# DMA transposes in place of TensorE transposes for most quantized rows of a feed-forward part, and the down product half a step later

## The reference, cut to what matters

```python
def _act_quant(x):
    scale = 127.0 / jnp.clip(jnp.max(jnp.abs(x), axis=-1, keepdims=True), 0.0001, None)
    y = jnp.clip(jnp.round(x * scale), -128, 127) / scale
    return x + jax.lax.stop_gradient(y - x)

def _linear_bit(x, w, g):
    xq = _act_quant(_rmsnorm(x, g))          # g * x * rsqrt(mean(x*x) + 1e-8)
    wq = _ternary_quant(w)
    return jnp.einsum('bsd,od->bso', xq, wq)

swish = jax.nn.silu(_linear_bit(x, w1, g1))   # w1, w2: 2048 x 512
h = swish * _linear_bit(x, w2, g2)
return _linear_bit(h, w3, g3)                 # w3: 512 x 2048
# around it: x = x + tanh(g_ffn[0]) * ffn(layernorm(x))
```

## Time and profile before

| | us |
|---|---|
| median of 3 runs (lowest to highest) | 655.0 (654.78 to 655.46) |
| the profiled execution | 656.19 |
| its span, first to last instruction | 654.4 |
| busy: TensorE / VectorE / ScalarE / GpSimd | 635.1 / 536.5 / 422.2 / 360.2 |
| HBM read / written | 45.16 MB / 2.10 MB |

### The profile page before, as it was taken

One profiled execution on the slowest core, in us unless ns is written; L12 is line 12 of the kernel. 1 busy time (PEld: TensorE's weight loads), 2 busy tenths in 40 slices (PEclk: granted clock), 3 DMA queues, 4 the chain that ended last, 5 costly groups with the idle time before them and its releaser, 6 DMA issues.

```text
span 654.4 us, 9986 instructions
## 1 busy us (share of the span) xinstructions
PE 635.1 (97%) x2968; PEld 394.0 (60%) x2968; DVE 536.5 (82%) x870; ACT 422.2 (65%) x693; POOL 360.2 (55%) x304
## 2 busy tenths in 40 slices
PE   8789999999999999999999999999999998999997
PEld 7555466766766676666666666566656554545553
DVE  4778787788878877887789978997899987998863
ACT  2564686477737764776567766776666633598875
POOL 4722376655545554565367854664457144686651
PEclk9999999999999999999999999999999999999999
DMA  8207976788589858984988798878689872000001
GB/s 283 87 6 188 274 196 164 206 223 240 151 227 241 219 131 239 251 224 106 251 222 221 201 242 224 222 195 231 169 221 251 198 177 81 1 1 33 17 35 48
DMA packets 45208, 112.79 MB, mean 172 GB/s; under 512 B 11888, under 2 KB 15088, under 8 KB 45040
## 3 DMA queue, kind: packets, MB, share of 16 engines
q1 hardware_dynamic: 42128, 104.24, 60.1%
q10 hardware_dynamic: 2976, 8.06, 4.0%
q0 software_dynamic: 64, 0.00, 0.0%
HBM read 45.16 MB, written 2.10 MB: 72 GB/s over the span
## 4 chain that ended last, share of the span: by engine, by line
PE 68%; DVE 10%; SPq 8%; ACT 4%; issue 4%; DMA 3%; POOL 1%; PEld 1%; POOLq 0%; ACTq 0%; DVEq 0%; PEldq 0%
PE ps_s L1443 11%; SPq L1132 8%; PE ps_b L1476 6%; PE ps_s L623 5%; PE ps_ctx L1476 5%; PE ps_b L1339 4%; PE ps_b L1394 4%; DMA G<-E 3%; PE ps_b L1341 3%; PE ps_b L1413 3%; PE ps_b L1340 3%; ACT E L1675 2%; PE ps_b L674 2%; DVE small L1858 2%; PE ps_ctx L1472 2%
## 5 line engine op out<-in xcount | busy, mean ns | idle before, releaser
L1675 ACT ACTIVATE E<-ps_s,small 128x1024 f32<-128x1024 f32 x128 | 142.5, 1116 | 143.4 <-DVE small L1858 110.5
L1241 POOL TENSOR_TENSOR G_lo<-G,g_hi 128x512 fp32r<-128x512 f32 x130 | 168.0, 1306 | 117.7 <-ACT g_hi L1619 117.7
L1858 DVE TENSOR_REDUCE small<-ps_s 128x1 f32<-128x1024 f32 x128 | 149.8, 1211 | 34.5 <-PE ps_s L1443 34.3
L1872 DVE STREAM_TRANSPOSE E<-E 128x1024 f32<-128x1024 f32 x124 | 152.0, 1230 | 0.1
L1199 POOL TENSOR_SCALAR E<-E,small 128x1024 f32<-128x1024 f32 x64 | 78.9, 1233 | 109.6 <-DVE small L1864 98.0
L1619 ACT ACTIVATE g_hi<-G 128x512 fp32r<-128x512 f32 x130 | 76.9, 631 | 3.5 <-DVE wq L1888 3.5
L1339 PE MATMUL ps_b<-b_hi,ctx_hi 128*128 128x512 f32 x128 | 66.8, 522 | 0.3 <-DVE ctx_lo L1818 0.3
L1476 PE MATMUL ps_b<-G,kv 128*128 128x512 f32 x126 | 63.7, 600 | 1.7 <-DMA G<-E 1.7
L1476 PE MATMUL ps_ctx<-G,kv 128*128 128x512 f32 x126 | 64.6, 607 | 0.1
L1443 PE MATMUL ps_s<-k_hi,q_hi 64*128 64x512 f32 x256 | 57.3, 444 | 3.8 <-ACT E L1675 2.6
L623 PE MATMUL ps_s<-wq,q12T 128*128 128x512 fp8e4 x256 | 59.8, 379 | 0.1
(11 more groups left out here) (203 smaller groups left out, 1211.7 us busy)
## 6 DMA issues: line engine op xcount, KB each, us to landing
G<-E SPq DMA_DIRECT2D x496, 128.0 KB, 2.6
w_stage<-in_wffn SPq DMA_DIRECT2D x37, 512.0 KB, 4.8
w_stage<-in_wffn ACTq DMA_DIRECT2D x11, 512.0 KB, 4.4
wo_s<-in_woT SPq DMA_DIRECT2D x8, 512.0 KB, 5.4
wq_s<-in_wq SPq DMA_DIRECT2D x7, 512.0 KB, 5.5
wkcq_s<-in_wkcqT SPq DMA_DIRECT2D x7, 384.0 KB, 3.4
out<-x_sb SPq DMA_DIRECT2D x8, 256.0 KB, 2.0
x_sb<-in_x SPq DMA_DIRECT2D x3, 512.0 KB, 6.3
```

Of the source, the lines that this page charges most:

```text
L1241: nc.gpsimd.tensor_tensor(g_tile(w % 2, i, G_lo), tile, high_part(i).bitcast(F32).rearrange("p (t i q) -> p t i q", t=ST, i=4), ALU.subtra ...
L1675: nc.scalar.activation(out, scores, ACT.Exp, bias=negmax[:, k:k + 1], accum_out=rowsum[:, k:k + 1]).then_inc(exp_done, 1)
L1858: nc.vector.tensor_reduce(negmax[:, k:k + 1], ps_s[:, t % 2, :], AX_X, ALU.max, negate=True).then_inc(max_done, 1)
L1872: nc.vector.transpose(e_tile(w % 2, t), e_tile(w % 2, t)).then_inc(blocks_turned, 1)
```

## The change

Rows of tiles 2 to 7 and hidden rows of tiles 0 to 5 are no longer turned by TensorE. ScalarE widens the integers to bfloat16 in place (`widen_rows`, 1024 columns, where the copy of turned rows stood; `widen_hidden`, 2048 columns, right behind the rounding and ahead of the square), and SyncE issues one transposing transfer within SBUF for each (`turn_rows`, `turn_hidden`), in the order rows 2, rows 3, hidden 0, rows 4, hidden 1, and so on, with the stores between them. The down product of tile `t - 3` stands after chunk 1 of step `t`; before, that of tile `t - 2` stood at the end of step `t`. VectorE's read of it moves from the end of its step to the place ahead of product 3. The tail is turned on TensorE as before. The scales `h_deq` get a column for each tile.

```diff
+            def turn_rows(t):
+                sp.wait_ge(q12_wide, t - FIRST_MOVED + 1)
+                sp.wait_ge(up_done, HC * (t - 1))
+                sp.dma_start_transpose(q12T[:, t % 2, :, :, :].rearrange("p i c s -> p (i c) s"),
+                                       qn12[:, t % 2, :, :].rearrange("p i d -> p (i d)").bitcast(BF16)).then_inc(q12_moved[t % 2], 16)
+            def turn_hidden(t):
+                sp.wait_ge(q3_wide, t + 1)
+                if t >= 2:
+                    sp.wait_ge(mm3_done, t - 1)
+                sp.dma_start_transpose(q3T[:, t % 2, :, :], qn3[:, t % 2, :].bitcast(BF16)).then_inc(q3_moved[t % 2], 16)
+            for t in range(1, TT):
+                if t + 1 < TT:
+                    turn_rows(t + 1)
+                if t >= 2:
+                    turn_hidden(t - 2)
+                if t >= 4:
+                    store(t - 4)
...
         def gate_up(pe, t, k, c):
-            pe.wait_ge(q12T_ready, 2 if early and c == 1 else t + 1)
+            if t < FIRST_MOVED:
+                pe.wait_ge(q12T_ready, 2 if early and c == 1 else t + 1)
+            else:
+                pe.wait_ge(q12_moved[t % 2], 16 * (t // 2))
...
-                    if turn and c == 0:
-                        turn_rows(pe, t, k)
-                    if out and c in T3_AT:
...
-                            last = nc.tensor.transpose(t3[:, a, b, :], qn3[:, k, (8 * a + b) * P:(8 * a + b + 1) * P].bitcast(BF16), identb[:, :])
-                if out and not (isinstance(t, int) and t == LAST):
...
+                    if t >= 3 and c == DOWN_AT:
+                        down(t - 3)
+            def down(t):
+                pe.wait_ge(q3_moved[t % 2], 16 * (t // 2 + 1))
+                pe.wait_ge(side_read, t + SIDE_READ0)
+                for f in range(FF // P):
...
+        def widen_rows(act, t):
+            act.wait_ge(q12_ready, t + 1)
+            rows = qn12[:, t % 2, :, :].rearrange("p i d -> p (i d)")
+            copy_act(rows.bitcast(BF16), rows).then_inc(q12_wide, 1)
+        def widen_hidden(act, t):
+            act.wait_ge(q3_ready, t + 1)
+            rows = qn3[:, t % 2, :]
+            copy_act(rows.bitcast(BF16), rows).then_inc(q3_wide, 1)
...
                     if turn and c == 0:
-                        turned_rows(act, t, k)
-                    if out and c in T3_AT:
...
+                        widen_rows(act, t + 1)
...
                 if t == 1:
                     silu(act, 2, 0, 0)
+                    widen_hidden(act, 0)
                     norm_act(act, 2, 0)
-                elif mm:
+                else:
+                    widen_hidden(act, t - 1)
                     hidden_square(act, t, k)
...
                     chunk_max(dve, t, k, 1)
+                    down_read(t - 3)
                     product(dve, t, k, 3)
```

More of the change, by code:

```diff
@@ L528, in ffn_sp, with store @@
             sp.dma_start(g3, A["g3"].partition_broadcast(P)).then_inc(ld_g3, 16)
-            with sp.Fori(0, TT) as t:
+            def store(t):
                 sp.wait_ge(side_read, t + (SIDE_READ0 + 1))
-                sp.dma_start(out_dram[:, bass.ds(t, 1), :], x_sb[:, bass.ds(t, 1), :]).then_inc(stored, 16)
+                sp.dma_start(out_dram[:, t:t + 1, :], x_sb[:, t:t + 1, :]).then_inc(stored, 16)
+            def turn_rows(t):
[15 more added lines that the diff above has]
+                    store(t - 4)
+            for t in range(LAST_MOVED - 1, TT):
+                store(t)
             sp.wait_ge(stored, 16 * TT)
@@ L658, in step @@
                             pe_last_out(pe, s)
-                    if turn and c == 0:
-                        turn_rows(pe, t, k)
-                    if out and c in T3_AT:
[L662 to L666, removed]
-                            last = nc.tensor.transpose(t3[:, a, b, :], qn3[:, k, (8 * a + b) * P:(8 * a + b + 1) * P].bitcast(BF16), identb[:, :])
-                        last.then_inc(t3_done, 1)
-                if out and not (isinstance(t, int) and t == LAST):
[L670 to L676, removed]
+                    if t >= 3 and c == DOWN_AT:
[4 more added lines that the diff above has]
+                for f in range(FF // P):
+                    last = nc.tensor.matmul(ps_side, q3T[:, t % 2, f, :], wq8[:, 2 * DT + f // 4, (f % 4) * NF:(f % 4 + 1) * NF],
+                                            start=(f == 0), stop=(f == FF // P - 1))
+                last.then_inc(mm3_done, 1)
             def turn_half(t, a):
                 pe.wait_ge(q3_half, 2 * (t - (LAST - 1)) + a + 1)
-                pe.wait_ge(et_free, 2 * t + (a - 1 + ET_FREE0))
+                pe.wait_ge(et_free, ET_FREE0 + (a + 1 if t == LAST else 0))
                 for b in range(8):
@@ L790, in step @@
                 if quant:
-                    if not (isinstance(t, int) and t < 3):
-                        act.wait_ge(t3_done, 2 * t - 4)
+                    if t >= 3:
+                        act.wait_ge(q3_moved[(t - 3) % 2], 16 * ((t - 3) // 2 + 1))
                     act.wait_ge(hfac_chain, HCH * t)
@@ L932, in norm_quant @@
             scales(dve, y_am[:, 2 * k:2 * k + 2], fs[:, bass.ds(t + 10, 1)], y_fac[:, 2 * k:2 * k + 2], yfac_chain, 3 * t + 6)
-            if not (isinstance(t, int) and t < 0):
+            if 0 <= t < FIRST_MOVED:
                 dve.wait_ge(t12_done, t + 1)
+            elif t >= FIRST_MOVED:
+                dve.wait_ge(q12_moved[t % 2], 16 * (t // 2))
             for i in range(2):
@@ L1079, in step @@
                     chunk_max(dve, t, k, 3)
-                if out and not (isinstance(t, int) and t == LAST):
-                    dve.wait_ge(mm3_done, t - 1)
-                    dve.wait_ge(hdeq_ready, t - 1)
-                    x = x_tile(t - 2)
-                    nc.vector.scalar_tensor_tensor(x, ps_side, h_deq[:, k:k + 1], x, ALU.mult, ALU.add).then_inc(side_read, 1)
             product(dve, 0, 0, 3)
```

31 lines of the change are left out of this document (14 added, 17 removed).

## The result

| | before | after |
|---|---|---|
| median of the runs, us | 654.89 (653.38 to 655.46, 6 runs) | 659.46 (657.49 to 659.85, 6 runs) |
| ratio, 95% interval | | 1.0066 (1.0051 to 1.0081) |
| profiled execution: time, span, us | 656.19, 654.4 | 659.71, 657.9 |
| TensorE busy, us | 635.1 | 628.1 |

The account below looks back on a forecast made before the run. TensorE's 11.70 us step was taken as the bound, with a ring of 11.58 through GpSimd, VectorE and ScalarE just under it. Terms +2.6, +1.2 and +1.3 sum to +5.1, taken as +5.0 on 655.0: 660.0 us, range 656.5 to 668.

Parts of the forecast that it names:

- The bound: Feed-forward steps: TensorE, busy in all 11.70 us, drops to 10.37 a step and disappears under the ring's 12.24.
- the ring: Chain from GpSimd's row gains through VectorE and ScalarE back to GpSimd; one turn 11.58 us, TensorE's step only 0.12 longer.
- First turns: Up to step 3: ScalarE's early hidden widenings move GpSimd's gains from 585.46 to 588.6.
- Steady turn: Steps 4 and 5: distance between GpSimd's gains goes from 11.58 to 12.24 us, 12.5 where the widening adds its 0.3.
- the widening's 0.3 a turn: ScalarE between rounding and square: the hidden widening uses up the 0.88 us wait and some 0.3 more in steady steps.
- the read's 0.66: VectorE's read of the down product, now between chunk 1's maximum and product 3, adds 0.66 us to each turn.
- TensorE's busy time: Removing 18 batches of eight transposes at 0.45 us each takes 8.1 us off TensorE.
- The start of step 6 and the tail: Step 6's first chunk starts 2.6 us later; from there TensorE's work adds 1.2 and its waits 1.3.
- The transfers: SyncE's row and hidden-row transfers: 3 and 5 us, within 6.0 for rows and 9.7 for both, at no cost.
- Rival (A): SyncE's transfers miss their deadlines and its queue sets the step, 12.2 to 16 us; 671 us, chance 0.15.
- (B): Faster: VectorE's wait absorbs the read, widenings take half or less, turn below 11.3; about 651 us, chance 0.08.
- (C): No difference: widening 2048 columns on ScalarE takes 0.5 to 0.8 us, the read's 0.66 stays; 655 to 656.3, chance 0.06.

Follow-up runs that it names:

- The widening put into before: Kernel before with one added ScalarE copy of the rounded hidden rows (2048 columns) between rounding and square in steps 2 to 6; 657.13 us, ratio 1.0048.
- the control: Changed kernel with its twelve transposing transfers replaced by plain copies of the same sizes, so rows are not turned; 658.97 us, ratio 1.0066.
- the widening alone: As the control, with each hidden row widened in two halves behind the silus of chunks 1 and 2 of the next step; 656.98 us, ratio 1.0029.
- the hidden half alone: Changed kernel with only hidden rows moved (plain copies, not turned), rows 2 to 7 turned by TensorE; 663.89 us, ratio 1.0150.
- the two kernels above: As the control, with each moving transfer issued twice, or four times; 660.44 us and 660.99 us, ratios 1.0087 and 1.0092.
- only rows moved: Kernel before with only rows 2 to 7 moved to SyncE (plain copies, not turned); 654.06 us, ratio 0.9995.
- the mixed one: Kernel before with rows 2 to 7 and hidden rows 4 and 5 moved (plain copies, not turned), nothing put on the ring; 652.49 us, ratio 0.9971.
- The run with the late read: As the control, with VectorE's read of the down product behind product 3 instead of ahead of it; 660.81 us, ratio 1.0095.

## Why the prediction was right, and where its terms were not

**The bound.** Right. TensorE's work went from 11.70 to 10.4 a step, and the step went to 12.2 and 12.4, the ring's turn.

**First turns.** Predicted 3.1 late at step 3, measured 2.9 (table). The experiments give it to the widening whole: split, it takes 2.9 us off at that place. The widening put into before, which has only the second of the two, makes that turn 13.85 for 12.11, which is 1.7 of the 2.9; the other 1.2 is there at step 2 already, where the gains start 12.99 us after the common point (573.43) for 11.81 in before.

**Steady turn.** Predicted 12.24 and 12.5, measured 12.22 and 12.38. The number is right and its make-up is not. I priced the read at 0.66 and gave the widening some 0.3 on top. The runs show two strands side by side that meet at the square: VectorE's with the read is 0.65 longer than in before (12.22 without the widening), ScalarE's with the widening 0.54 to 0.73 (12.11 and 12.31 without the read on it, 12.11 and 12.14 in before with the operation added). The turn is about the longer of the two (0.65 and 0.80 with both), not their sum of 1.2 to 1.4. The step that failed is the widening's 0.3 a turn, under-sized by about half and put behind the read's 0.66 where it lies beside it. The two errors nearly cancel, so that the turn came out well is in part luck. Where they don't cancel, the error shows: by the prediction's terms the read's move alone was to bring 1.3 to 2 us, and it brought nothing.

**TensorE's busy time.** Predicted 8.1 less, measured 7.0. Some of the difference is in the chunks behind an idle time, whose 16 matmuls are shown as 3.8 us for 3.62; what else there is stays open. The time does not hang on it.

**The start of step 6 and the tail.** Predicted +2.6 and then +2.5, measured +2.4 and +2.4. The stall before down product 5 was to be 1.5 and is 1.48 at 642.14, with VectorE's read as its releaser.

**The transfers.** Assumed 3 and 5 us, measured 3.2 and 4.4, and no cost: the control has the same ratio. Rival (A), missed deadlines, is out: no wait of TensorE in the changed kernel ends with a transfer, and even four copies of everything brought one such wait, of 0.78. Both rules that I weighed can be read now: 8 blocks of 128x128 land in 3.2 us and 16 in 4.4, or 0.40 and 0.28 us a block from issue to landing. *VectorE: DVE Perf Modes* (The three transpose paths) of the Trainium skill has 1309 ns for one; paid block by block that does not hold here. *Advanced Engine Details and Errata* (X-Bar Transpose) of the Trainium skill has transposing transfers as fast as regular ones; plain copies of the same size landed in 2.3 and 3.1, so here a transposing transfer takes 1.4 times as long from issue to landing, and the measurement decides; for this kernel the difference cost nothing.

**Rivals (B) and (C).** (B) needed the 1.13 us wait to absorb the read; it stayed at 1.09. (C) needed a widening of 0.5 to 0.8; it is 1.91. Without the hidden widening, and with plain copies, the kernel is level with before (654.95), near (C)'s 655 to 656.3.

## What to carry to other kernels

When TensorE's step is 0.1 us above a ring through the other engines, offloading TensorE is worth 0.1 us, and whatever the offload adds to the ring's longest strand is lost in full; list what each engine has between two points where they meet, and take the longest strand, not the sum. Undoing one of two equal strands shows nothing, so remove both before you call either innocent. An offload's by-products (a conversion, a read that changes its place) belong where an engine waits anyway: in halves behind two silus the same widening cost 0.5 us at most (L = 90.42, against 89.95 with the widening left out). And when TensorE starts to wait, look at its granted clock in each profiled execution before two of them are compared: a fall was worth 1.3 to 1.7 us here, as much as the read.

## What the runs showed of the hardware

- Widening 16-bit integers to 16-bit floats inside SBUF on ScalarE takes 1.91 us for 2048 columns and 1.04 for 1024, as long as squaring 2048 columns of 32-bit data (1.90): narrower data was no faster. *ScalarE: Activation LUTs* (What ACT_TABLE_LOAD costs) of the Trainium skill has 186 ns and 0.833 ns a column, for 16-bit floats and 32-bit floats alike; by these figures 2048 columns are an estimated 1.89 us. The 1.91 measured agrees, though the input here is 16-bit integers, and the estimate speaks against rival (C).
- Issuing a transposing transfer holds SyncE's queue for 1.23 to 1.25 us (256 KB) and 1.8 to 3.0 us (512 KB) in the changed kernel; in the control, issuing the plain copies holds it for 0.46 to 0.51 and 0.47 to 0.59.
- Where TensorE idled 2.0 us or more, its granted clock fell to 0.50 for some microseconds in some executions and not in others. The profiled execution of the change has idle times of 2.10 and 2.45 and kept 1.00, and so did the control behind 2.44. The control's fell in 580 to 582 us at no cost: the turn was 13.82 there, and 13.84 in the change at 1.00, as the ring set the time. Where TensorE's work was on the path, a fall cost 1.3 to 1.7 us (the widening alone in the tail, the hidden half alone, the two kernels above). Before, whose longest wait in the steps is 0.5, kept 1.00 there, and so did the kernels with only rows moved, with the widening put into before and the mixed one, whose longest is 1.2.
- The run with the late read scatters from 657.5 to 663.1, and why is open. Its slowest execution has the lowest mean clock of the five (0.992), but the mean is 0.997 at 657.52 as well as at 662.56, so the clock is not all of it.
